# Scores of the second query tile from three fp32r products, in a fused cross-attention, attention and mixture-of-experts kernel

## What is computed

```
q = (h @ wq + bq) ; k = (h @ wk + bk) ; v = (h @ wv + bv)      # each to b, head, s, 128
q = q * cos + rotate_half(q) * sin
k = k * cos + rotate_half(k) * sin
scores = einsum('bhqd,bhkd->bhqk', q, k) / sqrt(128)
scores = where(causal, scores, min) ; probs = softmax(scores)
out = einsum('bhqk,bhkd->bhqd', probs, v) -> b, s, 2048 ; return out @ wo + bo
```

## Time and profile before

| | |
|---|---|
| median of 3 runs | 525.49 us (520.78 to 527.2) |
| the profiled execution | 523.37 us |
| its span, first to last instruction | 521.5 us |
| mean granted TensorE clock | 0.986 of full speed |
| start of the scores of unit 0 | 166.46 us |
| steps 4 to 57 (one each) | 184.94 to 425.22 us |
| end of the profiled span | 521.5 us |

### The profile page before, as it was taken

How to read it: one execution, slowest core, us unless ns; L and a number is a source line. 1 busy time by engine, 2 the same in 40 slices (tenths; PEclk the granted TensorE clock), 3 DMA queues, 4 the chain that set the end, 5 groups by cost and what they waited for, 6 DMA issues and landing times.

```text
span 521.5 us, 10743 instructions
## 1 busy us (share of the span) xinstructions
PE 462.1 (89%) x3316; PEld 418.4 (80%) x3316; DVE 376.3 (72%) x1179; ACT 269.7 (52%) x725; POOL 234.3 (45%) x318
## 2 busy tenths in 40 slices
PE   0159999989976799999999999999999998589996
PEld 0149999978855589999999999999999997578895
DVE  4876578785655787877878787788887778944544
ACT  2048877767511255565655645555556557263342
POOL 7944424921024644544544645446355431161251
PEclk9999999999998999999999999999999999997899
DMA  8100000020002434334243243352442320000011
GB/s 288 17 3 2 1 1 2 5 79 1 3 20 62 96 67 121 83 80 134 57 136 77 60 141 80 80 141 60 101 120 60 80 62 1 1 1 1 1 41 41
DMA packets 19882, 31.42 MB, mean 60 GB/s; under 512 B 6020, under 2 KB 8200, under 8 KB 19848
## 3 DMA queue, kind: packets, MB, share of 16 engines
q1 hardware_dynamic: 15928, 22.31, 17.5%
q10 hardware_dynamic: 3920, 8.69, 5.5%
HBM read 13.16 MB, written 1.05 MB: 27 GB/s over the span
## 4 chain that ended last, share of the span: by engine, by line
PE 76%; DVE 14%; ACT 4%; issue 4%; DMA 2%; POOL 0%; SPq 0%; DVEq 0%; ACTq 0%; POOLq 0%
PE bank L1195 40%; PE bank L1148 6%; PE bank L1275 5%; PE bank L1238 5%; PE bank L1266 4%; PE bank L1131 3%; PE bank L1276 2%; PE bank L1237 2%; ACT PR L515 2%; PE bank L1100 1%; PE bank L1122 1%; PE bank L1079 1%; DMA cst_sb<-in_cst 1%; DVE small L656 1%; PE bank L1354 1%
## 5 line engine op out<-in xcount | busy, mean ns | idle before, releaser
L411 POOL TENSOR_TENSOR room<-room,qk_room 128x512 f32<-128x512 f32 x64 | 82.4, 1288 | 104.6 <-DMA qk_room<-qk_room 104.6
L555 ACT ACTIVATE PR<-sm,nm 128x128 f32<-128x128 f32 (+1 forms) x128 | 57.2, 448 | 117.3 <-DVE nm L927 117.3
L1195 PE MATMUL bank<-hH,qk_parts 128*128 128x512 f32 x256 | 81.2, 399 | 0.0
L850 DVE SCALAR_TENSOR_TENSOR qk_room<-bank,qk_bias,cst_sb 128x512 f32<-128x512 f32 x64 | 48.0, 750 | 37.5 <-PE bank L1195 33.6
L1195 PE MATMUL bank<-hL,qk_parts 128*128 128x512 f32 x128 | 62.0, 485 | 9.2 <-DVE room L850 6.1
L1195 PEld LDWEIGHTS bank<-hH,qk_parts 128*128 128x128 f32 x256 | 48.7, 190 | 9.9
L515 ACT ACTIVATE PR<-bank,nxm 128x128 f32<-128x128 f32 (+1 forms) x128 | 45.8, 435 | 14.7 <-DVE nxm L820 12.4
L1148 PE MATMUL bank<-PTs,room 128*128 128x128 f32 x384 | 50.7, 276 | 0.1
L850 DVE SCALAR_TENSOR_TENSOR room<-bank,qk_bias,cst_sb 128x512 f32<-128x512 f32 x64 | 47.5, 743 | 0.0
L1148 PEld LDWEIGHTS bank<-PTs,room 128*128 128x128 f32 x384 | 46.6, 192 | 0.3 <-ACT PTs L231 0.3
L1195 PE MATMUL bank<-woH,o_parts 128*128 128x256 f32 x256 | 46.5, 280 | 0.0
(11 more groups left out here) (198 smaller groups left out, 1271.2 us busy)
## 6 DMA issues: line engine op xcount, KB each, us to landing
qk_room<-qk_room SPq DMA_DIRECT2D x128, 128.0 KB, 2.3
stg<-in_wqkv ACTq DMA_DIRECT2D x6, 768.0 KB, 4.6
stge<-in_we ACTq DMA_DIRECT2D x7, 256.0 KB, 3.4
stg<-in_wqkv SPq DMA_DIRECT2D x2, 768.0 KB, 6.4
stgo<-in_wo ACTq DMA_DIRECT2D x6, 256.0 KB, 3.8
x_sb<-in_x SPq DMA_DIRECT2D x4, 256.0 KB, 6.3
out_y<-yacc SPq DMA_DIRECT2D x4, 256.0 KB, 2.1
cst_sb<-in_cst SPq DMA_DIRECT2D x1, 520.0 KB, 7.1
```

Of the source, the lines that this page charges most:

```text
L411: pool.tensor_tensor(v, v, qk_sw[:, q, :], ALU.subtract).then_inc(s["rope_done"], 1)
L555: ins = act.activation(PR[:, q, a:e], sm[:, q, a:e], ACT.Exp, bias=nm[:, q, t:t + 1], scale=-1.0, accum_out=rs[:, q, t:t + 1])
L850: return dve.scalar_tensor_tensor(out.rearrange("p (b t) -> p b t", b=2), O_B[q][:, :].rearrange("p (b t) -> p b t", b=2), qk_bias[:, c:c ...
L1195: ins = pe.matmul(outp, l, r, start=(m == 0), stop=(m == n - 1))
```

## The change

A new tile `split_room` of fp32r holds a high and a low part of the roped keys of all positions (`k_split`) and of the roped queries of the second query tile alone (`q_split`). ACT makes the high part of each chunk (`roped_high`) and POOL the low part (`roped_low`): 128 x 512 for a chunk of k (c odd), and 128 x 256, in two runs of 128, for a chunk of q (c even). The second product of `scores` (128 x 256 out) becomes `three` on these parts. The first product stays plain float32. PE now waits for `split_low` where it waited for `rope_done`. In step T, ACT does `roped_high` of chunk T + 4 after its copy of v and before its weight parts, and POOL does `roped_low` of chunk T + 4 after `rope_add` of chunk T + 6, last in the step. Chunks 0 to 3 are split ahead of the loop.

```diff
+        split_room = sb("split_room", [P, 2, 3 * NT * P], F32R)
+        k_split = split_room[:, :, 0:2 * NT * P].rearrange("p m (r n) -> p m r n", r=2)
+        q_split = split_room[:, :, 2 * NT * P:3 * NT * P].rearrange("p m (r b n) -> p m r b n", r=2, b=B)
...
+        def to_split(c, g):
+            v = QT[:, c, 512 * g:512 * (g + 1)]
+            if c % 2:
+                return (v, *(k_split[:, m, c // 2, 512 * g:512 * (g + 1)] for m in range(2)))
+            return (v.rearrange("p (b t n) -> p b t n", b=2, t=2)[:, :, 1, :], *(q_split[:, m, c // 2, 2 * g:2 * g + 2, :] for m in range(2)))
...
@@ gpsimd
+            def roped_low(n, c, g):
+                pool.wait_ge(s["split_high"], n + 1)
+                v, high, low = to_split(c, g)
+                pool.tensor_tensor(low, v, high.bitcast(F32), ALU.subtract).then_inc(s["split_low"], 1)
...
             for n in range(LEAD):
                 rope_add(n, 32 * (n // 2 + 1), n % 2, n % 4, n // 4)
+                if n in (1, 3):
+                    roped_low(n - 1, n - 1, 0)
+                    roped_low(n, n, 0)
                 if n == 1:
                     hidden_low(B - 1)
...
                 if unit(i, j, -LEAD):
                     c, g = chunk_at(j)
                     rope_add(U * i + j + LEAD, 32 * (4 * i + (j + LEAD) // 2 + 1), j % 2, c, g)
+                if unit(i, j, -4):
+                    roped_low(U * i + j + 4, j % 4, (j + 4) // 4 % 2)
...
@@ scalar
+            def roped_high(n, c, g):
+                act.wait_ge(s["rope_done"], n + 1)
+                v, high, _ = to_split(c, g)
+                act.activation(high, v, ACT.Copy).then_inc(s["split_high"], 1)
...
             v_out(1, 1)
+            roped_high(0, 0, 0)
+            roped_high(1, 1, 0)
             h_high(B - 1)
             v_out(2, 2)
+            roped_high(2, 2, 0)
+            roped_high(3, 3, 0)
...
                     v_out(B * i + m, m % B)
+                if unit(i, j, -4):
+                    roped_high(T + 4, j % 4, (j + 4) // 4 % 2)
                 if more and j < 4:
...
@@ tensor
-                pe.wait_ge(s["rope_done"], U * i + 4 * (j // 4) + 2 * r + 2)
+                pe.wait_ge(s["split_low"], U * i + 4 * (j // 4) + 2 * r + 2)
...
                 pe.matmul(S_B[j % 2][:, 0:P], QT[:, 2 * r, first], QT[:, 2 * r + 1, first], start=True, stop=True)
-                pe.matmul(S_B[j % 2][:, P:3 * P], QT[:, 2 * r, second], QT[:, 2 * r + 1, both], start=True, stop=True).then_inc(s["b_s"], 1)
+                three(S_B[j % 2][:, P:3 * P], [([q_split[:, m, r, b, :] for m in range(2)],
+                                                [k_split[:, m, r, 256 * b:256 * (b + 1)] for m in range(2)])]).then_inc(s["b_s"], 1)
```

More of the change, by code:

```diff
@@ L160, in build_kernel @@
         nh_ready yacc_init hT_ready hH_ready h_ready we_half we_ready
-        wqk_ready wqk_half wqk_bias wv_ready wv_half wo_ready wo_half b_recip c_gmax c_gexp c_gdiff chunk_pe chunk_sin chunk_cos rope_done bv_ready
+        wqk_ready wqk_half wqk_bias wv_ready wv_half wo_ready wo_half b_recip c_gmax c_gexp c_gdiff chunk_pe chunk_sin chunk_cos rope_done split_high split_low bv_ready
         b_s b_max b_exp b_norm b_pt b_ptcopy b_pv b_oH b_oL b_wo b_yadd v_pe v_ready
@@ L1232, in scores @@
                 b, r = j // 2, j % 2
-                pe.wait_ge(s["rope_done"], U * i + 4 * (j // 4) + 2 * r + 2)
+                pe.wait_ge(s["split_low"], U * i + 4 * (j // 4) + 2 * r + 2)
                 if unit(i, j, 2):
                     pe.wait_ge(s["b_max"], T - 1)
-                first, second, both = (slice(256 * b + x, 256 * b + y) for x, y in ((0, P), (P, 2 * P), (0, 2 * P)))
+                first = slice(256 * b, 256 * b + P)
                 pe.matmul(S_B[j % 2][:, 0:P], QT[:, 2 * r, first], QT[:, 2 * r + 1, first], start=True, stop=True)
-                pe.matmul(S_B[j % 2][:, P:3 * P], QT[:, 2 * r, second], QT[:, 2 * r + 1, both], start=True, stop=True).then_inc(s["b_s"], 1)
+                three(S_B[j % 2][:, P:3 * P], [([q_split[:, m, r, b, :] for m in range(2)],
+                                                [k_split[:, m, r, 256 * b:256 * (b + 1)] for m in range(2)])]).then_inc(s["b_s"], 1)
             pe.wait_ge(s["h_ready"], 3)
```

## The result

The change made the kernel slower: 534.82 us against 525.62 us for the kernel before in the same session (medians of six executions each), ratio 1.0185 with the 95% interval [1.0133, 1.0236]. So it is slower than before beyond doubt, but the interval holds 2%. The ratio is that of the means and leaves out two slow executions, one of after (2576.86 us) and one of before (530.14 us). The profiled execution of after took 533.39 us around a span of 531.6. I read it in the order in which I had read that of before.

A forecast was written before the change was run, and what follows sets the result against it. PE alone was taken to bound steps 4 to 57. PE's gain -4.5, steady waits +3.2, start +1.5 and end +3.4 sum to +3.6 us, so 525.49 becomes 529.1 us; range 521 to 536, chance of the forecast 0.6.

The forecast's parts named there:

- PE's gain: Second score product on PE: three fp32r products save 0.08 us a unit in some 57 units, -4.5 us.
- The start: First units: unit 1 waits for low parts of chunks 2 and 3, rope chain delayed, +1.5 us.
- the upper case: Start: PE waits for the rope chain, where POOL has about 3.2 us a step against 2.4; high end 3 us.
- The steady waits: Steps 4 to 57: PE's scores wait for POOL's low part of chunk T + 2, +3.2 us.
- The wait at j = 5: Scores at j = 5, such as unit 21: low part 0.54 us late, 6 times, +3.2 us.
- Step 7 is just in time: Pass 2, ahead of unit 25 (j = 1): the low part is ready in time by 0.1 us.
- The end: Last steps: unit 60 is 0.4 us late, unit 61 gets +3.9; +3.4 us reach the end.
- The first (the waits don't come): Whole kernel: gain comes through, waits don't, about 1 us of costs left at start and end; 522.0 us, chance 0.2.
- The second: Step 7: its swap meets a weight load and lands late, 1.5 us in six passes, +9, 538 us; chance 0.1.
- The third: Even steps: POOL's k low part holds DVE's normalisation, 0.8 us in 30 steps, +24, 553 us; chance 0.05.
- The rule quoted in the prediction: Trainium skill: GpSimd shares SBUF interfaces with VectorE, contends with 2-port modes and two-input instructions; that rule alone gives 553.
- The fourth: Score products on PE: the fp32r group saves nothing, 533.6 us; chance 0.05.

The follow-up runs named there:

- e1_gain_alone: Changed kernel without high and low parts or the wait for them; three products read parts filled once with constants: 520.54 us, ratio 0.9937 to before.
- e2_unused: Changed kernel making all high and low parts, but PE uses the plain product and waits for rope_done only: 531.77 us, ratio 1.0138 to before.
- e6_two_columns: Changed kernel with every wait and order kept, but each low part made for two columns of each run only: 524.33 us, ratio 1.0002 to before.
- e8_low_first_start: e4_low_first with chunks 0 to 3 split one at a time, each right behind its rope: 525.97 us, ratio 1.0047 to before.
- e9_plain_start: e8_low_first_start with chunks 0 to 3 not split and the plain product for units 0 to 3: 527.29 us, ratio 1.0031 to before.
- e5_end_order: Changed kernel with the last low part of wo put behind the split in the step before last: 531.66 us, ratio 1.0168 to before.
- e4_low_first: Changed kernel splitting chunk T + 5 in step T, not T + 4, and ahead of rope_add: 526.62 us, ratio 1.0032 to before.
- e7_one_input: Changed kernel with each low part made by a one-input copy, except two columns still subtracted: 526.78 us, ratio 1.0043 to before.
- e12_wait_for_norm: e8_low_first_start with one added wait: at j = 3 and 4 POOL lets DVE normalise first: 531.87 us, ratio 1.0116 to before.
- e11_rope_halves: e9_plain_start with the low part of k and rope_add each cut into two instructions of 256 columns: 528.97 us, ratio 1.0070 to before.

## Why the prediction was off where it was

The range held the result and the sign was right, but 529.1 was 5.7 us too low. By its own steps:

**PE's gain: right.** Forecast 0.08 us for 57 units, -4.5; measured 0.07 for 54 units, -3.9 (e1_gain_alone). The three units more that I counted brought nothing in sum: the end of e1_gain_alone is 0.08 us shorter than that of before.

**The start: right in size by luck.** Forecast +1.5, measured +1.54. I had taken it from the late unit 1, 1.8 us behind its low parts. But unit 1 came only 0.47 us later behind unit 0 than before, with no wait for the split, and partly at the clock of 0.50 that I had not counted. e2_unused, in which no unit waits for the split, has +2.4, and e6_two_columns, with short low parts, has +0.1. So it is the length of POOL's low parts, by POOL's time in the rope's chain, which I had named as the upper case, and by the normalisations that it holds, for which I had counted nothing. e8_low_first_start and e9_plain_start did not get it back.

**The steady waits: right in place, wrong in price, and with two terms missing.** The wait at j = 5 came in six passes as forecast, at 0.3 to 0.4 us a step and not 0.54. The order was right: ACT's high part moved `low_qk` by 0.5 to 0.6 us against PE's step (forecast 0.53). PE's release took 0.05 us and not the 0.15 that I had put without a row; the rest is that the low part ended at 4.62 us of the step in most passes, where my times put it at 4.76. At j = 0 and 1 there was about 1.3 us in all. "Step 7 is just in time" was read from pass 2 alone. In pass 0 the swap of chunk 12 landed late, and POOL had the experts' part and a `rope_add` (206.84 and 208.08) ahead of the low part of k: unit 9's step took 6.10 us against 4.43, 1.7 us from one place. The trace of before has the same order there, with that `rope_add` over at 206.5 and unit 9 at 207.17, so it was there to be read. The rest, at the units behind j = 5 and in step 2, is 0.1 here and there. Over the pure gain's 236.42 these are 6.4 us, where I had 3.2.

**The end: the step that failed by size.** Forecast +3.4, measured +5.74. Unit 60 is 0.57 late (forecast 0.4) and unit 61 3.57 more (forecast 3.9 in all), so order and prices held. The term that was too small is what I took from these to the end: I took back 0.5 for slack that did not come, and counted nothing for the clock, which fell to the lower level behind PE's idle time of 3.41 us: unit 62 came 1.49 later than its 3.13. e5_end_order shows both: 1.7 us less wait and the clock kept.

**The rivals.** The first (the waits don't come) is what e4_low_first makes true in the steady stretch. The second fell: from pass 2 on the steps at j = 1 are 4.36 to 4.52 us, and none shows 1.5 more. The late swap of pass 0 is in the trace of before too. The third was too small in my account. I had counted nothing for DVE held by POOL, because DVE's idle 0.93 us a step would cover it. On average it does: 26.8 us of longer normalisations brought nothing like the 24 us of the rival as stated. But the cover fails where a hold meets a chunk that is wanted next. That is shown for the long steps at j = 5, 0.7 to 0.8 us of the 2.1 to 2.4 that the steady stretch keeps in e8_low_first_start and e4_low_first, and for the start, where PE waited longer for normalisations than before. For the rest of these stretches, and for e2_unused's 7.9 us over before in the medians, the share of the holds is not measured. The rule quoted in the prediction thus held in kind: the two engines do contend. The fourth fell with e1_gain_alone.

What stays open: how much of the start and of e2_unused's end (+2.3 us) is POOL's time and how much DVE's holds. Both show in the trace of its start, but no run takes away one alone; e7_one_input changes both at once.

## What to carry to other kernels

An engine that is idle for half of the time is not free: ask how long its instructions are beside the chain that feeds the bound engine, which queue they stand in, and whom they hold while they run. Before you call an added instruction hidden, check every pass, the first and the last above all, where steps are short or loads differ. Order is cheaper to mend than work: making the split a step earlier and ahead of the rope's sum gave back 8 of 9 us with the same instructions. But a wait or a move must be followed through each engine and back, as e12_wait_for_norm shows.

## What the chip showed that I had not expected

- A DVE normalisation that starts just behind a POOL instruction lasts until that one ends, 1.39 us in place of 0.35 behind a sum of two inputs of 512 columns, and 0.64 in place of 0.29 behind a copy of one input of 510. Between two shorter POOL instructions in a row it is let through (0.95 us at most in e11_rope_halves), but then more normalisations are held.
- The granted clock went to 0.50 for 3.4 us after PE's idle time of 3.41 us and came back by itself, here with PE busy all the time. It also fell after 2.31 us of waiting in e6_two_columns, whose step from unit 61 to 62 took 4.69 us, and not after 2.89 us in e7_one_input or 1.68 us in e5_end_order, both with a step of 3.07. So the length of one wait doesn't decide it alone; what does was not settled.
- Going from a plain float32 product to fp32r ones and back costs nothing that shows: 0.07 us a unit were saved in e1_gain_alone, of 0.08 by the prices of the products alone.
